# Second cross attention of a two-layer decoder: per-head weights folded before the stage, value rows passed through DRAM, scores and output as full-height products

## What is computed

```python
N_HEAD, MODEL_DIM, KEY_DIM, VALUE_DIM = (16, 128, 64, 64)
residual = query                                   # x: 64 x 128 tokens x 128
q = (query @ Wq + bq).reshape(b, sq, N_HEAD, KEY_DIM)
k = (key @ Wk + bk).reshape(b, key.shape[1], N_HEAD, KEY_DIM)     # context: 64 x 77 tokens x 128
v = (value @ Wv + bv).reshape(b, value.shape[1], N_HEAD, VALUE_DIM)
scores = jnp.einsum('bqhd,bkhd->bhqk', q, k) / TEMP
attn = jax.nn.softmax(scores, axis=-1)
out = jnp.einsum('bhqk,bkhd->bqhd', attn, v).reshape(b, sq, N_HEAD * VALUE_DIM)
out = out @ Wo + bo + residual
mu = jnp.mean(out, axis=-1, keepdims=True)
var = jnp.var(out, axis=-1, keepdims=True)
return (out - mu) * jax.lax.rsqrt(var + EPS) * ln_gamma + ln_beta
```

## Time and profile before

| | before |
|---|---|
| time, three runs | 3138.29, 3137.42, 3138.17; median 3138.17 us |
| span of the profiled execution | 3137.1 us |
| outside the span (median less span) | 1.1 us |
| stage s, from its opening to the opening of c | 1052.4 to 2050.8 us |
| stage c, from its opening to its last statistics | 2050.8 to 2873.9 us |
| stage q | from 2874.2 us to the end |
| PE busy over the span | 85% |
| length of one step of c in the middle | 12.42 us |

### The profile page before, as it was taken

One profiled execution on the slowest core, in us unless ns is written; L12 is line 12 of the kernel. 1 busy time (PEld: TensorE's weight loads), 2 busy tenths in 40 slices (PEclk: granted clock), 3 DMA queues, 4 the chain that ended last, 5 costly groups with the idle time before them and its releaser, 6 DMA issues. The chain is left out here.

```text
span 3137.1 us, 50219 instructions
## 1 busy us (share of the span) xinstructions
PE 2676.3 (85%) x16584; PEld 1602.4 (51%) x16584; DVE 2419.8 (77%) x3997; ACT 1705.7 (54%) x3208; POOL 2031.9 (65%) x1795
## 2 busy tenths in 40 slices
PE   7969999899799478888888887689999999996655
PEld 5646666566466223333333333247777777774222
DVE  5979999466344699999999999967677676666887
ACT  7847777443222365666666666434444444444665
POOL 5549999477466389999999999723433434333454
PEclk9979999899899689999998999899999999998555
DMA  5911110011455443443333434200000000000000
GB/s 194 382 22 23 23 23 15 21 42 42 123 161 154 124 180 128 156 148 145 150 138 149 152 132 157 86 17 3 5 3 5 3 5 5 3 3 1 14 20 20
DMA packets 130013, 249.45 MB, mean 80 GB/s; under 512 B 41041, under 2 KB 97894, under 8 KB 109170
## 3 DMA queue, kind: packets, MB, share of 16 engines
q1 hardware_dynamic: 119106, 228.72, 21.5%
q0 software_dynamic: 9088, 16.94, 1.6%
q10 hardware_dynamic: 1584, 0.79, 0.1%
HBM read 189.08 MB, written 59.13 MB: 79 GB/s over the span
## 5 line engine op out<-in xcount | busy, mean ns | idle before, releaser
L1774 POOL TENSOR_TENSOR s_drive<-s_du,s_b_sb 128x1024 f32<-128x1024 f32 x256 | 599.8, 2359 | 29.4 <-DVE s_state_ps L2089 29.0
L2197 PE MATMUL s_y_ps<-s_read,w_ident 128*128 128x512 f32 x832 | 447.5, 668 | 156.5 <-DVE s_read L2102 156.3
L2089 DVE TENSOR_TENSOR_SCAN s_state_ps<-s_decay_ps,s_drive 128x512 f32<-128x512 f32 x416 | 486.8, 1215 | 43.9 <-ACT s_decay_ps L1926 33.7
L1926 ACT ACTIVATE s_decay_ps<-s_delta,neg_rate 128x508 f32<-128x508 f32 x512 | 345.6, 684 | 288.6 <-DVE s_state_ps L2089 239.3
L2197 PEld LDWEIGHTS s_y_ps<-s_read,w_ident 128*128 128x128 f32 x832 | 157.9, 203 | 415.3 <-DVE s_read L2102 258.0
L2449 ACT ACTIVATE c_pT<-c_turn_ps 77x512 f32<-77x512 f32 x256 | 148.8, 587 | 243.5 <-PE c_turn_ps L2682 243.5
L2102 DVE TENSOR_TENSOR s_read<-s_state_ps,s_c_sb 128x1024 f32<-128x1024 f32 x208 | 254.6, 1224 | 7.2
L2394 POOL TENSOR_TENSOR c_p<-c_p,c_norm 128x1232 f32<-128x1232 f32 x64 | 143.9, 2249 | 151.4 <-DVE c_norm L2553 151.4
L2372 POOL TENSOR_TENSOR x<-c_xs,w_c_bo 128x128 f32<-128x128 f32 x64 | 30.9, 484 | 292.0 <-DVE c_xs L2513 292.0
L1421 POOL DMA_INDIRECT m_y_scratch<-e_y,e_index x156 | 152.7, 979 | 95.2 <-DVE e_y L1467 53.3
L742 ACT ACTIVATE b_pT<-b_turn_ps 77x512 f32<-77x512 f32 x256 | 144.6, 592 | 73.9 <-PE b_turn_ps L871 73.9
(11 more groups left out here) (375 smaller groups left out, 6896.9 us busy)
## 6 DMA issues: line engine op xcount, KB each, us to landing
s_b_sb<-s_bc_scratch SPq DMA_DIRECT2D x64, 1024.0 KB, 4.7
s_c_sb<-s_bc_scratch SPq DMA_DIRECT2D x64, 1024.0 KB, 4.7
m_rows_scratch<-fill SPq DMA_DIRECT2D x33, 1040.0 KB, 27.2
e_w<-in_m_we_dram SPq DMA_DIRECT2D x39, 384.0 KB, 3.3
e_xg<-m_rows_scratch SPq DMA_DIRECT2D x39, 260.0 KB, 3.5
s_read<-m_y_scratch SPq DMA_DIRECT2D x32, 256.0 KB, 3.4
out_dram<-q_result SPq DMA_DIRECT2D x16, 256.0 KB, 2.3
x<-in_x_dram SPq DMA_DIRECT2D x13, 256.0 KB, 2.8
```

Source lines behind the costliest of these rows:

```text
L1774: nc.gpsimd.tensor_tensor(drive[:, (g * states + n) % drives, :, :], du[:, s, :, :], b_sb[:, n, :].unsqueeze(1).broadcast_to([128, halves, ...
L1926: nc.scalar.activation(decay[:, m, :, 1:], delta[:, s, m, :].rearrange("p (b t) -> p b t", t=T)[:, :, 1:], ACT.Exp, scale=core.neg_rate[:, ...
L2089: nc.vector.tensor_tensor_scan(home[:, h, :], decay[:, h, :, :].rearrange("p b t -> p (b t)"), drive[:, (g * states + n) % drives, h, :], ...
L2197: last = nc.tensor.matmul(y_ps[:, m, :], core.ident[:, :], read[:, r % deep, m, :], start=False, stop=False)
```

## The change

Two products of weights are formed once, at the opening of stage s, in PSUM that the scan does not use yet: per head `Wq_h Wk_h^T` (with x's mean subtraction and 1/128 of the query bias in it), a 128 x 128 matrix, and per head `Wv_h Wo_h`, a 128 x 128 matrix. The value bias goes through `Wo` into the output bias.

Stage c then has no query product. A key product per head turns the 308 context rows of a group with the folded matrix (16 per group, 4 per step); the scores of an element are 4 products of 128-high x by 4 x 77 columns. The values of a context token are now 16 x 128 numbers. They are made for 128 tokens at a time, irrespective of elements (39 lots with 4 products of 512 columns each, 156 in all, spread evenly over 64 steps), taken by ScalarE to `made` (two slots), written by SP to DRAM with the rows of an element ordered by head and token, and read back as ten lumps of 128 rows (the last has 80) into `vp` (three slots), two DMAs per element. The 16 x 77 probabilities of a token are transposed as ten blocks of 128, and ten products with `vp` add up to the finished output. VectorE no longer adds biases; ScalarE takes every projection. Probabilities have three slots instead of two.

```diff
+    rows = heads * S2
+    lumps = -(-rows // 128)
+    lots = -(-B * S2 // 128)
+    parts = heads * 128 // 512
-    ahead_x, ahead_turn, ahead_qk, ahead_v = 10, 9, 5, 2
+    begin, ahead_x, ahead_turn, ahead_k, ahead_v = 8, 5, 4, 7, 2
+    p_slots, xT_slots, vp_slots, lot_slots = 3, 4, 3, 3
+        def made_by(i):
+            return max(0, min(lots * parts, -(-lots * parts * (i + begin + 1) // B)))
+        def pieces(j):
+            first, stop = 128 * j, 128 * j + lot_width(j)
+            return [(b, max(first, b * S2), min(stop, (b + 1) * S2)) for b in range(first // S2, (stop - 1) // S2 + 1)]
+        for i in range(-begin, B + 2):
+            fresh = list(range(made_by(i - 1), made_by(i)))
+            here = []
+            for n in range(4):
+                if n in (0, 1, 2) and n < len(fresh):
+                    here.append(("value", fresh[n]))
+                if on(i + ahead_k):
+                    here.append(("key", (i + ahead_k, n)))
...
+            if on(i + ahead_turn):
+                here.append(("x", i + ahead_turn))
...
+            plan[i] = (here[:2], here[2:cut], here[cut:])
         @block.sync
+            def store_lot(j):
+                done = value_no[parts * j + parts - 1]
+                sp.wait_ge(front_taken.sem, front_taken.at(done, 1))
+                for b, first, stop in pieces(j):
+                    sp.dma_start(
+                        vp_dram[b, :, :].rearrange("(h s) d -> s h d", s=S2)[first - b * S2:stop - b * S2, :, :],
+                        made[first - 128 * j:stop - 128 * j, j % 2, :].rearrange("s (h d) -> s h d", d=128)
+                    ).then_inc(lot_out[j % 2].sem, 16)
+            def load_values(i):
...
+                if i >= vp_slots:
+                    sp.wait_ge(y_ready.sem, y_ready.at(i - vp_slots, 1))
...
+                sp.dma_start(vp[:, i % vp_slots, 0:lumps - 1, :],
+                             vp_dram[i, 0:whole, :].rearrange("(c p) d -> p c d", p=128)).then_inc(slot.sem, 16)
+                sp.dma_start(vp[0:last_lump, i % vp_slots, lumps - 1, :],
+                             vp_dram[i, whole:rows, :]).then_inc(slot.sem, 16)
             def step(i):
...
+                for j in range(lots):
+                    if made_by(i - 2) < parts * j + parts <= made_by(i - 1):
+                        store_lot(j)
+                if on(i + ahead_v):
+                    load_values(i + ahead_v)
         @block.scalar
+            def take_value(unit):
+                mine = value_no[unit]
+                j, n = unit // parts, unit % parts
+                act.wait_ge(front_ready.sem, front_ready.at(mine, 1))
+                if n == 0 and j >= 2:
+                    act.wait_ge(lot_out[j % 2].sem, lot_out[j % 2].first + stored_upto(j - 2))
+                nc.scalar.activation(made[0:lot_width(j), j % 2, 512 * n:512 * (n + 1)],
+                                     f_ps[0:lot_width(j), mine % 2, :], ACT.Copy).then_inc(front_taken.sem, 1)
             def step(i):
+                if on(i):
+                    copy_p(i, 0)
+                    copy_p(i, 1)
+                take(early)
+                if on(i):
+                    copy_p(i, 2)
+                take(middle)
+                if on(i + 2):
+                    exp(i + 2)
+                take(late)
         @block.vector
             def step(i):
-                if on(i + ahead_qk):
-                    add_k(i + ahead_qk, 0)
-                    add_k(i + ahead_qk, 1)
-                if on(i + ahead_v):
-                    add_v(i + ahead_v)
         @block.tensor
+            def follow(number):
+                if number >= 2:
+                    pe.wait_ge(front_taken.sem, front_taken.at(number - 2, 1))
             def score(i):
+                for r in range(banks):
+                    last = nc.tensor.matmul(scores[:, r, :, :], xT[:, i % xT_slots, :],
+                                            k[:, g % 2, per * r:per * (r + 1), S2 * e:S2 * (e + 1)],
+                                            start=True, stop=True)
+            def mix(i):
+                slot = vp_in[i % vp_slots]
+                pe.wait_ge(slot.sem, slot.at(i // vp_slots, 32))
+                pe.wait_ge(pT_ready.sem, pT_ready.at(i, 3))
+                for c in range(lumps):
+                    last = nc.tensor.matmul(y_ps, pT[0:width(c), i % 2, c, :], vp[0:width(c), i % vp_slots, c, :],
+                                            start=(c == 0), stop=(c == lumps - 1))
             def step(i):
+                early, middle, late = plan[i]
+                if on(i + 2):
+                    score(i + 2)
+                if on(i):
+                    turn_p(i, 0)
+                    turn_p(i, 1)
+                make(early)
+                if on(i):
+                    turn_p(i, 2)
+                make(middle)
+                if on(i):
+                    mix(i)
+                make(late)
```

```diff
+            take_query(0)
+            take_query(1)
+            act.wait_ge(offset_ready.sem, offset_ready.at(0, 1))
+            nc.scalar.activation(core.w["c_bo"][:, :], decay[:, 0, 0, :], ACT.Copy).then_inc(offset_taken.sem, 1)
+            take_values(0)
             take_root(0)
+            act.wait_ge(bias_ready.sem, bias_ready.at(0, 1))
...
             normalise(0, 0)
+            take_keys(0)
             take_root(1)
```

More of the change, by code:

```diff
@@ new lines, in fold_bias @@
+            def fold_bias():
+                pe.wait_ge(query_taken.sem, query_taken.at(0, 2))
+                pe.wait_ge(offset_taken.sem, offset_taken.at(0, 1))
+                for h in range(2 * fold_blocks):
+                    b, rows = h // 2, head_rows(h)
+                    last = nc.tensor.matmul(decay[:, h % 2, 1, b:b + 1], wqk[rows, b, :],
+                                            core.w["c_bk"][rows, b:b + 1], start=True, stop=True)
+                last.then_inc(bias_ready.sem, 1)
@@ new lines, in fold_keys @@
+            def fold_keys(k):
+                pe.wait_ge(query_taken.sem, query_taken.at(0, 2))
+                if k >= 1:
+                    pe.wait_ge(keys_taken.sem, keys_taken.at(0, k))
+                for h in range(8 * k, 8 * k + 8):
+                    b, rows = h // 2, head_rows(h)
+                    last = nc.tensor.matmul(state[:, h % 2, 128 * (b % 4):128 * (b % 4 + 1)],
+                                            wqk[rows, fold_blocks + b, :], wqk[rows, b, :], start=True, stop=True)
+                last.then_inc(keys_ready.sem, 1)
@@ new lines, in fold_values @@
+            def fold_values(k):
+                if k >= 1:
+                    pe.wait_ge(values_taken.sem, values_taken.at(0, k))
+                for h in range(8 * k, 8 * k + 8):
+                    b, rows = h // 2, head_rows(h)
+                    last = nc.tensor.matmul(y_ps[:, h % 2, 128 * (b % 4):128 * (b % 4 + 1)],
+                                            wvo[rows, b, :], wvo[rows, fold_blocks + b, :], start=True, stop=True)
+                last.then_inc(values_ready.sem, 1)
+            centre_query(0)
@@ new lines, in step @@
+            def step(i):
+                for j in range(lots):
+                    if made_by(i + 1) <= parts * j < made_by(i + 2):
+                        load_lot(j)
+                if (i + ahead_k + 3) % GB == 0 and on(i + ahead_k + 3):
+                    load_group((i + ahead_k + 3) // GB)
+                for j in range(lots):
+                    if made_by(i - 2) < parts * j + parts <= made_by(i - 1):
+                        store_lot(j)
+                if on(i + ahead_v):
+                    load_values(i + ahead_v)
@@ L2440, in exp, with take @@
+            def take(units):
+                for kind, what in units:
+                    if kind == "value":
+                        take_value(what)
+                    elif kind == "key":
+                        take_key(*what)
+                    else:
+                        take_x(what)
             def exp(i):
                 act.wait_ge(lowered.sem, lowered.at(i, 1))
-                nc.scalar.activation(p[:, i % 2, :, :], p[:, i % 2, :, :], ACT.Exp,
+                nc.scalar.activation(p[:, i % p_slots, :], p[:, i % p_slots, :], ACT.Exp,
@@ new lines, in make_value @@
+            def make_value(unit):
+                j, n = unit // parts, unit % parts
+                mine = value_no[unit]
+                slot = lot_in[j % lot_slots]
+                pe.wait_ge(slot.sem, slot.at(j // lot_slots, 16))
+                follow(mine)
+                nc.tensor.matmul(f_ps[0:lot_width(j), mine % 2, :], lotT[:, j % lot_slots, 0:lot_width(j)],
+                                 core.w["c_wvo"][:, 4 * n:4 * n + 4, :].rearrange("p h d -> p (h d)"),
+                                 start=True, stop=True).then_inc(front_ready.sem, 1)
@@ L2656, in score, with make @@
+            def make(units):
+                for kind, what in units:
+                    if kind == "value":
```

(12 more changed lines are left out.)

459 lines of the change are left out of this document (230 added, 229 removed).

## The result

The changed kernel takes 3106.33 us (median of 4 runs, 3103.99 to 3107.72) where the kernel before took 3138.23 beside it (4 runs, 3137.42 to 3138.38): ratio 0.9899, 95% interval 0.9885 to 0.9913. That is 32 us less. The forecast was 65 us less, 3073, twice what came; 3106 lies inside the range of 2972 to 3150 and inside rival A's own, so the direction and the mechanism came out and the size was off by half. The profiled execution has a span of 3103.6 us.

The account below looks back on a forecast made before the run. PE was taken to bound stage c. From 3138.2 us, 149 less in stage c and 5 more for the fold gave 2994; 79 for late stores made 3073 us, range 2972 to 3150.

Parts of the forecast that it names:

- rival A: Stores in stage c: equal shares of whole rows, ACT stopped eight times; 3073 us, range 3045 to 3115, chance 0.50.
- the lateness of the stores: Stage c, stores of `made`: eight lots land late at 20.8 ns a packet on the first engine, 79 us in sum.
- the hand-overs: Stage c, projection banks between PE and ACT: 0.4 to 0.5 us on 9.8, a step of 10.2 us.
- the lead-in of stage c: Start of stage c: six leading steps of 4.2 to 4.6 us, then two of 6.6, before the full steps.
- The spread of the stores: Stores to DRAM: equal shares of whole token rows on as many engines as divide their count, at most 16.
- B: Rival for the stores: the same bytes spread evenly, nothing waits for DMA; 2994 us, range 2968 to 3020, chance 0.30.
- C: Rival for the stores: the first engine pays 26.1 ns or more a packet; 3138 us, 3165 at 27.8, chance 0.12.
- the clock: PE in stage c: waking at half clock behind each store wait adds up to 2 us apiece, left to the range.
- D: Rival in stage c: transfers hidden, hand-overs between PE and ACT make the step 11.3 us; 3056 us, chance 0.08.
- The fold: Opening of stage s: forming the folded weights delays the reciprocal, and the delay stays; +5 us, between 0 and +10.
- The scores at full height: Stage c scores: 4 products of 308 columns take 2.1 us, to 2.4; the half-high pairing had bought nothing.
- Covers: Stage c: ACT's 6.7 us, DVE below 8.7 and POOL's 5 are covered by PE's step of 10.2 us.

Follow-up runs that it names:

- e1: The changed kernel with each store piece cut into a multiple of 16 token rows and a rest; 3089.64 us, 3215.91 for the kernel before, ratio 0.9614.
- e8: The changed kernel with only lot 29's store pieces cut into a multiple of 16 rows and a rest; 3068.18 us, 3137.78 before, ratio 0.9775.
- e3: The changed kernel with each store piece cut in two, the first with the largest prime count of rows; 4329.59 us, 3215.91 before, ratio 1.3467.
- e6b: e1 with another order of a step's projection products, nothing added or removed; 3056.20 us, 3216.76 for the kernel before, ratio 0.9506.
- e9: The changed kernel with only the product order of e6b, stores untouched; 3084.28 us, 3137.78 for the kernel before, ratio 0.9826.
- e4: The changed kernel with contraction rows ordered by token then head, one store per lot; 3095.20 us, 3215.91 for the kernel before, ratio 0.9632.
- e10: e6b with ACT taking the first batch's root before the folded values in stage s; 2976.98 us, 3137.78 for the kernel before, ratio 0.9484.

## Why the prediction was right in kind and wrong in size

The mechanism of rival A came out. What failed are three terms of the sum, each too small: the lateness of the stores, 79 us for 91.4 (93.0 in the steps); the hand-overs, 0.4 us a step for 0.63; and the lead-in of stage c, 8.5 us too short. Together with a shorter tail they are the 33 us.

**The spread of the stores: right.** That each store goes in equal shares of whole token rows over as many engines as divide their count is shown from three sides: undone everywhere (e1, all waits gone), undone for one lot (e8, that lot's wait gone), made worse (e3, 37 waits). That the engine in question is the first of the sixteen is the rule's word; no view here names it. The Trainium skill (DMA: Bandwidth & Descriptors, Why a DMA increments its semaphore by 16 and not by 1) states this rule, and the traces agree: 22 GB/s and a share of 0.07 where by it one engine does the work. B (spread evenly) and C as a whole are out; B is what e1 makes true, and its 2994 would have been 3012.

**The failed term: the lateness of the stores.** I took 20.8 ns a packet, from two small transfers that differ by 24 packets an engine. Those rows can't carry it: they are given to 0.1 us, so their difference of 0.5 allows 16.7 to 25 ns, and b_ctxT's packets are 308 bytes (77 numbers), not 512. The stores of lots 5, 11, 17, 23 and 29, which queue behind nothing late, took 23.24, 32.09, 35.85, 32.31 and 49.65 us from the first issue to the end of ACT's wait. By a straight line through these that is 23.3 ns for each packet of the store alone and 2.1 us fixed, to within 0.9 us, and it agrees with the window at 22 GB/s and with e3. The same stores had 19.8, 20.1, 19.9, 24.7 and 18.9 us before ACT came to wait, so the windows of 19.8 and 24.5 were right but for lot 29's. A second part was wrong the other way: I put 127 packets of the read-backs into every store's window, and for these five lots the last read-back had been issued before the store, the next was issued behind it. With 23.3 ns the sum of the prediction is 105 us; without the 127 packets for the five it is 90, beside the 91.4 of the trace. So that 79 came as near as it did is in part luck, of two errors against each other. C's 26.1 ns is out, and the 17.7 ns, an estimate from the 27 GiB/s an engine of the Trainium skill (DMA: Bandwidth & Descriptors, Specifications), is further off than mine.

**The term left to the range: the clock.** From the third scores on, the 56 steps take 677.2 us; e1's take 584.2. The difference, 93.0, is 90.3 us of waits and 2.7 us more. That is a sum of both signs, not a small price each time. Set against e1's steps, lots 11 and 12 with 18.1 us of waits cost 21.8, lot 17 with 16.0 costs 18.1, and lots 23 and 24 with what follows, 17.9, cost 18.8; but lot 5 with 3.4 costs 1.3, and lots 29 and 30 with 34.9 cost 33.2. The half clock is there behind the standstills. Behind lot 29's (PE's timeline):

```profile
2645.24 1.37 PE L2834 MATMUL c_f_ps<-c_ctxT,w_c_wqk 128*128 128x308 f32 x2 [29.58 <-ACT c_made L2668]
2646.61 3.39 PE L2862 MATMUL c_s_ps<-c_k,c_xT 128*128 128x308 f32 x8
2649.84 1.04 PE L2878 MATMUL c_turn_ps<-w_ident,c_p 128*128 128x128 f32 x8
```

The granted clock is 0.50 to 2648 and 1.00 from 2650 on, and the scores take 3.23 us instead of 2.08. PE waits 29.6 us there where ACT waits 30.8: part of ACT's wait costs PE nothing. So "up to 2 us apiece" was the right order for single waits; what paid it back in others is not pulled apart.

**The failed term: the hand-overs.** The work of PE is 9.8 us a step as computed (e6b, with PE busy 100 in 100, has 9.87), but I put 0.4 us on it and it is 0.63. What I laid out by hand was right in its places and low in size; the step with three values, 11.0, I did not lay out. Over 56 steps 13.0 us. D is the same mechanism at nearly two and a half times the size. That it is the order of the products, and not issue or weight loads, e6b shows.

**The failed term: the lead-in.** I had six leading steps at PE's own pace (4.2 to 4.6) and two of 6.6. They are bound by the two banks going back and forth, for the most part:

```profile
2081.31 1.10 PE L2843 MATMUL c_f_ps<-w_c_wvo,c_lotT 128*128 128x512 f32 x2 [0.26 <-ACT c_made L2668]
2082.24 0.68 PE L2834 MATMUL c_f_ps<-c_ctxT,w_c_wqk 128*128 128x308 f32 x2
2083.18 1.10 PE L2843 MATMUL c_f_ps<-w_c_wvo,c_lotT 128*128 128x512 f32 x2 [0.26 <-ACT c_made L2668]
```

A value and a key start every 1.87 us where they are 1.39 of work. The first four products of the stage, at a granted clock of 0.84 and 0.82, take 5.31 us where four of 0.87 are 3.5. First scores come at 2091.86 where 2086.5 was forecast (with the fold), and the two steps behind them are 8.49 and 7.85: 8.5 us in all to the third scores. That all of it lies behind the first product is luck. It came at 2057.83, and 2053 with 5 us of fold is 2058; but the kernel before had its own at 2055.6, not near 2053, and here PE stood 4.8 us for its context:

```profile
2057.83 5.40 PE L2843 MATMUL c_f_ps<-w_c_wvo,c_lotT 128*128 128x512 f32 x8 [4.78 <-DMA c_lotT<-in_ctxT_dram]
```

**The sum of it.** Lead-in +8.5, full steps +13.0, waits with the clock behind them +14.0 (93.0 for 79), tail -2.7: +33, and 3073 + 33 = 3106. The chances have a slip: A, B and D alone are 0.88, so "faster" could not be 0.87.

**The fold.** The mechanism came out: the reciprocal is 1063.46 and waits 2.30 us for ACT's root; the first scan is 1117.48 instead of 1114.6, and since the stage opened 0.86 earlier, that is 3.7 us of delay for 5 forecast. What I had wrong is that it stays. Counted from the opening of stage s, the first product of c comes at 1003.2 before, 1006.3 in the changed kernel, and 1001.5 and 1001.6 in e8 and e9, whose stage s is the same program; over all ten traces with this stage s it is 1001.0 to 1008.5. The end of s moves by more than the fold costs, against a single trace of the kernel before, so the fold's price in the whole, from -2 to +5 us in these traces, is not settled.

**The scores at full height.** They cost 2.08 us where 2.1 was forecast, against 1.94 for the 16 half-high ones. The Trainium skill (TensorEngine Tiling (Array Packing), Theoretical Speedup) gives up to 2x for the half-high ones, by which they would be an estimated 3.9 at most; the trace is nowhere near that here. No run changed this alone.

**Covers.** DVE and POOL never closed a full step: e4 has three longer passes and the same full steps as e1.

Best of what was run: e10 and e6b, 160.8 and 160.6 us under the kernel before, 5% against the change's 1%.

## What to carry to other kernels

- Count the slowest dimension of every DMA, not its bytes: a store of 61 or 67 rows ran on one engine at 22 GB/s, and cutting every such store into a multiple of 16 and a rest gave 93 us for a handful of lines. A low GB/s beside a DMA share near 1/16 is how it looks in the windows.
- A slow DMA holds up whatever is behind it in its queue. More slots move the wait to the next client (`made`, then `vp`, then the context); repairing the transfer removes it.
- With two banks between PE and ACT, order the products so that a long one on ACT is not followed, two on, by one that needs its bank: 34 us here, with nothing added. With the late stores still there the same order gave 22, so mend these first.

## What the runs showed that I had not expected

- SP was stuck inside the issue of a DMA: 21.3 us for two stores on one engine and 25.0 for the next read-back, against 0.38. I had counted SP's issues and taken them as short. From the end of an issue to the landing the slow read-backs took 3.6 to 4.0 us, the quick ones 3.9 in the median: the whole delay lies in the issue. Why SP is held there no run shows.
- A stride of 16 floats costs DVE 2.26 us instead of 1.44 in a subtraction of 1232 columns and 2.24 instead of 1.44 in a sum, and POOL 2.80 instead of 2.25 for the product with the norm repeated on the outer dimension.
- A wait of ACT and what it costs are not the same: 3.4 us of waiting cost the steps 1.3 us, 18.1 cost 21.8, and 34.9 cost 33.2.
